# Loading one weight block from another engine's DMA queue, and reordering the first evictions, at the start of a Winograd-multiplied FFN kernel

## The chip, the cores and the metric

The kernel runs on one core of one Trainium2 chip. The metric is device time in microseconds (us) of one execution, the median of several runs. Engines are called as the profile does: PE (TensorE matmul), PEld (its weight loads), DVE (VectorE), ACT (ScalarE), POOL (GpSimd), SP (SyncE, which here only issues DMAs). "SPq" and "ACTq" are DMA issues on SP and on ACT.

## The reference, cut to what matters

```
xn = layernorm(x)                                   # x: 4 x 1024 x 1024, float32
g  = sigmoid(xn @ gate_w.T + gate_b); u_g = xn * g
s  = c * scan(b * u_g, tanh(a)) + (d + d_lr) * u_g  # d_lr from the mean of u_g over time
p  = softmax(xn @ wr.T); top 2 of 8; gates = p / sum
h  = silu(xn @ w1.T); h = silu(h @ w3.T); h = h @ w2.T
f[index_k] += gate_k * h       for the two choices k  # index_k is 0 to 7: a row of the output
out = x + s * silu(f)
```

The indices run from 0 to 7, so `f` differs from zero only in the first eight rows. The kernel computes the whole of `h` up to `silu(h @ w3.T)`, sums it by index, and applies `w2` to the eight sums; all other rows of `out` are copies of `x`.

## The kernel before, in words

Every product of a 1024x1024 weight with a unit of 1024 tokens is done with seven block products of 512x512 instead of eight, in sums and differences of blocks (the scheme of Strassen and Winograd). A unit `n` is 0 to 8: 0 to 3 multiply by `w1`, 4 by `gate_w`, 5 to 8 by `w3`. A product `i` of a unit is four tiles `j` of 128 rows, each accumulated in a bank of PSUM (`main0` to `main4`) over four slices `k`.

Each float32 factor is split in a high part, a rounded copy in the type float32r (`h..`, `wh..`, made on ACT), and a low part, the difference (`l..`, `wl..`, made on DVE). A product then is three matmuls, high by high, low by high and high by low: lines 995, 996 and 997, in `three`. So before PE can multiply anything, ACT must have copied and DVE subtracted.

The order of the work on all engines comes from one list, `steps`, written out by hand for the start and filled from a table afterwards. Each engine walks the same list and takes the steps that are its own, in that order, with semaphores between engines. DMA issues are steps, too: in the kernel before, all loads of the start are issued by SP (lines 717 to 734).

The steps around the change, all at the start, in unit 0:

- `WARM`: PE transposes the identity 34 times into the bank `spare` (line 1004); the results are not used.
- `ROW r`: SP loads 128 tokens, 512 KB, a "token tile" `r` (line 723). Tiles 0 and 1 go to `wh6f`, 2 and 3 to `wh5f`, 4 and 5 to `rows`, 6 and 7 to `wh4f`.
- `W0 k`: SP loads slice `k` of the first block of w1 (W11), 256 KB, into `wl2f` (line 726). `WL`: it loads a whole block, 1 MB (line 734).
- `NA`, `NB`: mean and variance of a token tile on DVE (1184 to 1186), the root on POOL, then the normalisation on DVE (1190). `NS` takes the mean and variance on ACT instead (859 to 861), for tiles 4 and 7.
- `TR t`: PE transposes a normalised tile in eight pieces (1014): four into one bank, four into another, `TE t,h` then evicts each of the two banks on ACT with two copies, high part (871) and float32 (873), and `TL t,h` makes the low part of it on DVE (1147, `x3r` and `x5r`).
- `WH0 k`: ACT makes the high part of slice `k` of W11 (877, `wh0r`), `WO0 k`: DVE its low part (1147, `wl0r`).
- `MP half,k`: PE multiplies two token tiles (256 columns) by slice `k` of W11: 12 matmuls. `MP 0,k` needs `WO0 k` and both `TL 0,0` and `TL 1,0`; `MP 1,k` needs `TL 3,0`.

From then on (`MM`, 512 columns each) PE has one product behind the other.

Of the kernel before, what the change touches and what calls it, by code (L numbers as in the profile page):

```python
# [5 lines left out]
P = 128  # L6
# [82 lines left out]
def plan():  # L89
# [7 lines left out]
    for n in range(NN):  # L97
# [93 lines left out]
        if 0 < n < GATE:  # L191
# [4 lines left out]
            for t, (m, i, j) in enumerate(when):  # L196
# [4 lines left out]
                if t % 4 == 3:  # L201
                    k = 4 * i + j
# [32 lines left out]
        if n >= GATE:  # L235
            for r in range(8):
                s = 8 * (n - GATE) + r
# [9 lines left out]
    for k in range(3):  # L247
# [7 lines left out]
    at(NN - 1, 6, 3, "FM", 0)  # L255
    at(NN - 1, 6, 3, "FM", 1)

    steps = [("WARM", 0), ("ROW", 0), ("ROW", 1)] + [("W0", k) for k in range(4)] + [("ROW", 2), ("ROW", 3), ("WL", 0, 6, "12"),
             ("ROW", 4), ("ROW", 5), ("ROW", 6), ("ROW", 7), ("WL", 0, 5, "21"), ("WL", 0, 4, "22"), ("CST", 0),
# [106 lines left out]
def program(nc, x, xT, wB, w2T, small, out):  # L366
    steps = plan()
# [14 lines left out]
    for s in steps:  # L382
        if s[0] == "XL":
            q = place[s[1:]]
# [25 lines left out]
    with ExitStack() as ctx:  # L410
# [33 lines left out]
        ident = sb("ident", [P, P])  # L444
# [17 lines left out]
        def w_f(p, part):  # L462
            return W[p][part][0][:, :, :]
# [29 lines left out]
        main = [ps(f"main{i}", [P, HT]) for i in range(BANKS)]  # L493
        lgp = [ps(f"lgp{i}", [P, HT]) for i in range(2)]
        spare = ps("spare", [P, HT])
# [6 lines left out]
        s_id = sem("s_id")  # L502
# [15 lines left out]
        s_w0 = [sem(f"s_w0{k}") for k in range(4)]  # L518
# [192 lines left out]
        @block.sync  # L711
        def _(eng):
            wait = Waiter(eng)
            ncopy = 0
            for s in steps:
                kind = s[0]
                if kind == "ROW":
                    r = s[1]
                    if r >= 10:
                        wait(s_st2, r - 9)  # L720
                    elif r >= 8:
                        wait(s_tr, 2 * (r - 3))
                    eng.dma_start(row_buf(r), x[r * P:(r + 1) * P, :]).then_inc(s_row[r if r < 8 else 4 + r % 2], 16)
                elif kind == "W0":
                    k = s[1]
                    eng.dma_start(w_f(2, 1)[:, k, :], wB[0, 0, 0, :, k, :]).then_inc(s_w0[k], 16)
                elif kind == "CST":
                    eng.dma_start(cst[:, :], small).then_inc(s_cst, 16)
                elif kind == "WL":
                    w, p, b = s[1:]  # L730
                    if w:
                        g = 7 * ((GATE, L2)[w - 1] - 1) + p
                        wait(s_mm, done(g))
                    eng.dma_start(w_f(p, 1), wB[w, int(b[0]) - 1, int(b[1]) - 1]).then_inc(s_wl[p], 16)
                elif kind == "XL":
                    n, b = s[1:]
                    kh, h = BLK[b]
                    vacated(wait, n, b)
                    if n < GATE:
                        src = xT[n, kh, h]  # L740
                    elif n == GATE:
                        wait(s_xs["acbd".index(b)], 16)
                        src = xh_d[kh, h]
                    else:
                        for j in range(4):
                            c_gone(wait, n - L2, AT_OF[(kh, h)], j)
                        src = H_d[n - L2, kh, h]
                    eng.dma_start(xf(n, b), src).then_inc(s_pl[loads[(n, b)][0]], 16)
                elif kind == "XS":
                    b = s[1]  # L750
                    raw_in(wait, 0, b)
                    kh, h = BLK[b]
                    eng.dma_start(xh_d[kh, h], xf(0, b)).then_inc(s_xs["acbd".index(b)], 16)
                elif kind == "MV":
                    wait(s_mvs, nth(*s))
                    eng.dma_start(mv_d[s[1]].rearrange("r (t p) -> (r t) p", p=P), mvs[:, :]).then_inc(s_mvd, 16)
                elif kind == "BC":
                    n, h = divmod(s[1], 2)
                    wait(s_mvd, 16 * nth("MV", s[1]))
                    if n > 1:  # L760
                        wait(s_ln, nth("LN", n - 1, "cd"[h]))
                    eng.dma_start(bcs[h][:, :, :], mv_d[s[1]].partition_broadcast(P)).then_inc(s_bc[h], 16)
                elif kind == "GL":
                    k = nth(*s) - 1
                    n, i, j = s[1:]
                    if k < 4:
                        wait(s_st2, 24)
                    else:
                        wait(s_gx, k - 3)
                    o, h = OUT_OF[i]  # L770
                    eng.dma_start(xt[:, k % 4, :], xh_d[o, h, :, j, :]).then_inc(s_xt[k % 4], 16)
                elif kind == "CP":
                    r0, r1 = max(E, s[1] * P), (s[1] + 1) * P
                    eng.dma_start(out[r0:r1, :], x[r0:r1, :]).then_inc(s_cp, 16)
                    ncopy += 1
                elif kind == "X8":
                    wait(s_oz, 1)
                    for q in range(NQ):
                        eng.dma_start(x8[rows8[q], :], x[0:E, q * QC:(q + 1) * QC]).then_inc(s_x8, 16)
                elif kind == "W2":  # L780
                    wait(s_mm, done(7 * (NN - 1) + 1))
                    for r in range(2):
                        eng.dma_start(w2f[:, 4 * r:4 * r + 4, :],
                                      w2T.rearrange("(k p) n -> p k n", p=P)[:, 4 * r:4 * r + 4, :]).then_inc(s_w2, 16)
            wait(s_fin, 1)
            for q in range(NQ):
                eng.dma_start(out[0:E, q * QC:(q + 1) * QC], fin[rows8[q], :]).then_inc(s_out, 16)
            wait(s_cp, 16 * ncopy)
            wait(s_out, 16 * NQ)
# [58 lines left out]
        def _(eng):  # L848
            wait = Waiter(eng)
# [12 lines left out]

            for s in steps:
                kind = s[0]
                if kind == "TE":
                    t, h = s[1:]
                    wait(s_tr, 2 * nth("TR", t) - 1 + h)
                    bk = tr_banks(t)[h][:, :].rearrange("p (k t) -> p k t", t=P)
# [5 lines left out]
                elif kind == "WH0":  # L874
                    k = s[1]
# [57 lines left out]
                elif kind == "ST":  # L933
# [3 lines left out]
                    q = s_ss[j] if i == 6 else s_sg[j] if i == 4 else s_su[j]  # L937
# [5 lines left out]
                elif kind == "STAT":  # L943
                    r = s[1]
                    k, h, t = nth(*s), r // 4 % 2, r % 4
# [45 lines left out]
        def _(eng):  # L991
# [7 lines left out]
            for s in steps:  # L999
                kind = s[0]  # L1000
                if kind == "WARM":
                    wait(s_id, 1)
                    for q in range(34):
                        eng.transpose(spare[:, q % 4 * P:(q % 4 + 1) * P], ident[:, :], ident[:, :])
                    wait(s_id, 2)
                elif kind == "TR":
                    t = s[1]
# [468 lines left out]
```

## Time and profile before

| | us |
|---|---|
| median of 3 runs | 775.17 |
| the three runs | 774.08, 775.17, 776.29 |
| the profiled execution, its own time | 776.75 |
| its span | 774.8 |
| PE busy | 756.1 (98%) |
| DVE busy | 510.9 (66%) |
| ACT busy | 347.4 (45%) |
| start of the first product (`MP 0,0`) | 15.43 |
| start of the fifth (`MP 1,0`) | 27.42 |

The profiled execution's own time holds its span and some 2 us around it. PE is busy nearly all the time, so time is to be had only where PE waits or runs slowly, and both happen in the first 28 us. "PEclk" is the clock that TensorE was granted: 1.00 is 2.4 GHz, 0.50 is 1.2 GHz. DMA rows give the packets of each queue: q1 is SP's, q10 ACT's.

### The profile page before, as it was taken

How to read it: one execution, taken by the hardware profiler on the slowest of the kernel's cores; microseconds unless marked ns; L12 is line 12 of the kernel's file. 1: busy time of each engine (PE TensorE's matmuls, PEld its weight loads, DVE VectorE, ACT ScalarE, POOL GpSimd, SP SyncE). 2: the span in 40 equal slices, each digit the busy share in tenths (PEclk: the TensorE clock that was granted, in tenths of full speed). 3: DMA queues.
4: the chain of work that ended last, by engine and by line, in shares of the span. 5: the costliest groups of instructions: out<-in, count | busy, mean ns of one | idle time of the engine just before them, and what ended most of it. 6: DMA issues, size and time to landing. Idle time of an engine off the chain costs nothing.

```text
span 774.8 us, 8825 instructions
## 1 busy us (share of the span) xinstructions
PE 756.1 (98%) x3544; PEld 596.9 (77%) x3544; DVE 510.9 (66%) x567; ACT 347.4 (45%) x451; POOL 40.3 (5%) x52
## 2 busy tenths in 40 slices
PE   5999999999999999999989999999999999999996
PEld 5868877887788787888878878778777778777773
DVE  5789789675958487557999998565534552455322
ACT  4769964835572434242834354225122332234121
POOL 3300103020302000000000000000000000000000
PEclk8999999999999999999999999999999999999999
DMA  8743774536442533566495613221230323010500
GB/s 333 273 164 139 239 236 162 203 137 213 154 150 95 191 136 123 217 207 254 155 384 174 273 47 135 110 113 78 109 136 28 162 110 135 1 55 2 217 1 3
DMA packets 27401, 117.21 MB, mean 151 GB/s; under 512 B 3440, under 2 KB 3680, under 8 KB 20320
## 3 DMA queue, kind: packets, MB, share of 16 engines
q1 hardware_dynamic: 18144, 99.87, 35.7%
q10 hardware_dynamic: 9216, 16.78, 5.8%
q8 instruction: 28, 0.46, 0.2%
q14 instruction: 13, 0.11, 0.0%
HBM read 95.60 MB, written 37.77 MB: 172 GB/s over the span
## 4 chain that ended last, share of the span: by engine, by line
PE 85%; DVE 8%; issue 3%; DMA 2%; ACT 2%; SPq 0%; DVEq 0%
PE main L995 27%; PE main L997 26%; PE main L996 26%; PE lgp L1061 2%; DMA wl6f<-wB 1%; PE spare L1088 1%; DMA wl2f<-wB 1%; PE lgp L1088 1%; DVE x3r L1147 1%; DVE s L1147 1%; DVE x3f L1147 1%; DVE x0r L1147 1%; DVE x1r L1147 1%; DVE u L1379 1%; PE main L1122 0%
## 5 line engine op out<-in xcount | busy, mean ns | idle before, releaser
L1147 DVE TENSOR_TENSOR s<-s,main 128x512 f32<-128x512 f32 x72 | 48.7, 682 | 62.7 <-PE main L997 62.6
L1147 DVE TENSOR_TENSOR u<-u,main 128x512 f32<-128x512 f32 x36 | 24.5, 685 | 49.5 <-PE main L997 49.5
L931 ACT ACTIVATE u<-u 128x512 f32<-128x512 f32 x32 | 20.1, 631 | 57.2 <-DVE u L1147 57.1
L931 ACT ACTIVATE s<-s 128x512 f32<-128x512 f32 x32 | 20.0, 630 | 52.5 <-DVE s L1147 52.5
L1147 DVE TENSOR_TENSOR u<-s,main 128x512 f32<-128x512 f32 x32 | 21.7, 682 | 29.6 <-PE main L997 29.6
L931 ACT ACTIVATE rows<-rows 128x512 f32<-128x512 f32 x16 | 10.1, 631 | 67.9 <-DVE rows L1147 67.8
L912 ACT ACTIVATE s<-main 128x512 f32<-128x512 f32 x36 | 20.5, 594 | 44.5 <-PE main L997 19.0
L1147 DVE TENSOR_TENSOR rows<-s,main 128x512 f32<-128x512 f32 x16 | 11.0, 687 | 31.2 <-PE main L997 31.2
L861 ACT ACTIVATE rows<-rows,nm 128x1024 f32<-128x1024 f32 x24 | 27.7, 1154 | 0.8
L859 ACT ACTIVATE rows<-rows 128x1024 f32<-128x1024 f32 x25 | 26.2, 1046 | 2.0 <-DMA rows<-x 1.8
L931 ACT ACTIVATE u<-main 128x512 f32<-128x512 f32 x32 | 18.6, 590 | 17.6 <-PE main L997 17.4
L995 PE MATMUL main<-x2r,wh0r 128*128 128x256 f32 (+1 forms) x48 | 16.8, 349 | 6.6 <-DVE x3r L1147 6.6
L997 PE MATMUL main<-x2r,wl0r 128*128 128x256 f32 (+1 forms) x48 | 16.3, 340 | 0.0
L995 PEld LDWEIGHTS main<-x2r,wh0r 128*128 128x128 f32 x48 | 10.2, 212 | 7.7 <-DVE x3r L1147 7.1
L845 POOL MEMSET tail<- 128x1024 f32 x1 | 1.0, 955 | 269.1 <-PE main L997 269.1
L833 POOL TENSOR_SCALAR mvu<-acs 128x4 f32<-128x4 f32 x6 | 5.0, 827 | 188.0 <-ACT rows L861 188.0
L996 PE MATMUL main<-x4r,wh4r 128*128 128x512 f32 x32 | 13.0, 406 | 0.0
L995 PE MATMUL main<-x6r,wh3r 128*128 128x512 f32 x32 | 12.5, 392 | 0.0
L996 PE MATMUL main<-x6r,wh0r 128*128 128x512 f32 x32 | 12.5, 390 | 0.0
L996 PE MATMUL main<-x5r,wh1r 128*128 128x512 f32 x32 | 12.5, 390 | 0.0
L997 PE MATMUL main<-x6r,wl3r 128*128 128x512 f32 x32 | 12.5, 389 | 0.0
L996 PE MATMUL main<-x5r,wh2r 128*128 128x512 f32 x32 | 12.5, 389 | 0.0
(699 smaller groups left out, 2440.0 us busy)
## 6 DMA issues: line engine op xcount, KB each, us to landing
out<-x SPq DMA_DIRECT2D x31, 512.0 KB, 7.3
rows<-x SPq DMA_DIRECT2D x26, 512.0 KB, 4.1
H_d<-u ACTq DMA_DIRECT2D x32, 256.0 KB, 4.3
H_d<-s ACTq DMA_DIRECT2D x16, 256.0 KB, 3.2
rows<-xh_d SPq DMA_DIRECT2D x16, 256.0 KB, 4.9
w2f<-w2T SPq DMA_DIRECT2D x2, 2048.0 KB, 10.5
wl6f<-wB SPq DMA_DIRECT2D x3, 1024.0 KB, 8.3
wl4f<-wB SPq DMA_DIRECT2D x3, 1024.0 KB, 7.3
```

Of the source, the lines that this page charges most:

```text
L833: eng.tensor_scalar(mvu[:, h, 0, :], acs[:, h, 0, :], 1.0 / D, None, ALU.mult)
L859: link(eng.activation(row, row, ACT.Copy, accum_out=total))
L861: return eng.activation(where, row, ACT.Square, bias=nm[:, 0:1], accum_out=square)
L912: eng.activation(s1[:, j, :], bk, ACT.Copy).then_inc(s_pa, 1)
L931: ins = eng.activation(dst, src, ACT.Silu)
L995: eng.matmul(o, sh, mh, start=first, stop=False, skip_group_check=True)
L996: eng.matmul(o, sh, ml, start=False, stop=False, skip_group_check=True)
L997: return eng.matmul(o, sl_, mh, start=False, stop=last, skip_group_check=True)
L1061: ins = eng.matmul(lgp[h][Q * q:Q * (q + 1), :], wr32[:, NQ * kh + q, :], xf(n, b)[:, q, :], start=(kh == 0), stop=(kh == 1))
L1088: ins = eng.matmul(acc[o][Q * j:Q * (j + 1), :], Pz[:, 8 * u + 4 * h + j, :], c_buf(n, i, j), start=(u == 0 and h == 0), stop=(u == NU - 1 ...
L1147: return eng.tensor_tensor(o, a, b, op)
L1379: ins = eng.scalar_tensor_tensor(buf, buf, 1.0, xt[:, k % 4, :], ALU.add, ALU.mult, accum_out=us[:, h, e:e + 1])
```

## The change

Three things change, all in the first steps.

1. The four `W0` loads are issued by ACT instead of SP, after a wait for the end of POOL's last preparation (`s_id` at 2, after `iota`). SP issues the token tiles right behind one another.
2. The order of ACT and DVE work: `WH0 2` and `WH0 3` go behind evictions, the low parts go between the `TL`, `NA 2` goes behind `TL 1,0`, and `TR 2` goes behind `MP 0,2`.
3. PE transposes the identity 38 times instead of 34 at the start, and 12 times more behind `TR 1`, into `main0`.

```diff
-    steps = [("WARM", 0), ("ROW", 0), ("ROW", 1)] + [("W0", k) for k in range(4)] + [("ROW", 2), ("ROW", 3), ("WL", 0, 6, "12"),
+    steps = [("WARM", 0)] + [("W0", k) for k in range(4)] + [("ROW", 0), ("ROW", 1), ("ROW", 2), ("ROW", 3), ("WL", 0, 6, "12"),
              ("ROW", 4), ("ROW", 5), ("ROW", 6), ("ROW", 7), ("WL", 0, 5, "21"), ("WL", 0, 4, "22"), ("CST", 0),
-             ("NA", 0), ("NA", 1), ("NB", 0), ("TR", 0), ("NB", 1), ("TR", 1),
-             ("WH0", 0), ("WH0", 1), ("WH0", 2), ("WH0", 3), ("TE", 0, 0), ("WO0", 0), ("TL", 0, 0), ("NA", 2), ("TE", 1, 0), ("TL", 1, 0),
-             ("TE", 0, 1), ("TE", 1, 1), ("WO0", 1), ("WO0", 2), ("NA", 3), ("NB", 2), ("WO0", 3),
-             ("MP", 0, 0), ("MP", 0, 1), ("TR", 2), ("MP", 0, 2), ("MP", 0, 3), ("NA", 5), ("NB", 3), ("TR", 3),
+             ("NA", 0), ("NA", 1), ("NB", 0), ("TR", 0), ("NB", 1), ("TR", 1), ("WARM", 1),
+             ("WH0", 0), ("WH0", 1), ("TE", 0, 0), ("WO0", 0), ("TL", 0, 0), ("WH0", 2), ("TE", 1, 0), ("WO0", 1), ("TL", 1, 0),
+             ("WH0", 3), ("TE", 0, 1), ("TE", 1, 1), ("NA", 2), ("WO0", 2), ("NA", 3), ("WO0", 3), ("NB", 2),
+             ("MP", 0, 0), ("MP", 0, 1), ("MP", 0, 2), ("TR", 2), ("MP", 0, 3), ("NA", 5), ("NB", 3), ("TR", 3),
...
-                elif kind == "W0":
-                    k = s[1]
-                    eng.dma_start(w_f(2, 1)[:, k, :], wB[0, 0, 0, :, k, :]).then_inc(s_w0[k], 16)
...
+                if kind == "W0":
+                    k = s[1]
+                    wait(s_id, 2)
+                    eng.dma_start(w_f(2, 1)[:, k, :], wB[0, 0, 0, :, k, :]).then_inc(s_w0[k], 16)
...
-                    for q in range(34):
-                        eng.transpose(spare[:, q % 4 * P:(q % 4 + 1) * P], ident[:, :], ident[:, :])
+                    idle = main[0] if s[1] else spare
+                    for q in range(12 if s[1] else 38):
+                        eng.transpose(idle[:, q % 4 * P:(q % 4 + 1) * P], ident[:, :], ident[:, :])
```

How the instructions stand on ACT, from the program's start, before the change (`wh0r<-wl2f` are the high parts of W11, the rows with `main`, `lgp` and `spare` the evictions of token tiles 0 and 1):

```order
L877 ACT_TABLE_LOAD
L877 ACTIVATE wh0r<-wl2f 128x512 x4
L871 ACTIVATE x2r<-main 128x4x128
L873 ACTIVATE x0f<-main 128x4x128
L871 ACTIVATE x2r<-lgp 128x4x128
L873 ACTIVATE x0f<-lgp 128x4x128
L871 ACTIVATE x4r<-lgp 128x4x128
```

And with the change:

```order
L865 DMA wl2f<-wB 128x512 x4
L878 ACT_TABLE_LOAD
L878 ACTIVATE wh0r<-wl2f 128x512 x2
L872 ACTIVATE x2r<-main 128x4x128
L874 ACTIVATE x0f<-main 128x4x128
L878 ACTIVATE wh0r<-wl2f 128x512
L872 ACTIVATE x2r<-lgp 128x4x128
L874 ACTIVATE x0f<-lgp 128x4x128
L878 ACTIVATE wh0r<-wl2f 128x512
L872 ACTIVATE x4r<-lgp 128x4x128
```

The four loads now stand ahead of everything on ACT, the load of the function table too, and two of the four high parts stand ahead of the first eviction instead of four.

DVE in the same place, from the normalisation of tiles 0 and 1 on, before:

```order
L1190 TENSOR_SCALAR wh6f<-wh6f,mv 128x1024 x2
L1147 TENSOR_TENSOR wl0r<-wl2f,wh0r 128x512
L1147 TENSOR_TENSOR x3r<-x0f,x2r 128x4x128
L1184 BN_STATS bst<-wh5f 128x6
L1185 BN_STATS bst<-wh5f 128x6
L1186 BN_AGGR mv<-bst 128x2
L1147 TENSOR_TENSOR x3r<-x0f,x2r 128x4x128
L1147 TENSOR_TENSOR wl0r<-wl2f,wh0r 128x512 x2
```

And with the change:

```order
L1192 TENSOR_SCALAR wh6f<-wh6f,mv 128x1024 x2
L1149 TENSOR_TENSOR wl0r<-wl2f,wh0r 128x512
L1149 TENSOR_TENSOR x3r<-x0f,x2r 128x4x128
L1149 TENSOR_TENSOR wl0r<-wl2f,wh0r 128x512
L1149 TENSOR_TENSOR x3r<-x0f,x2r 128x4x128
L1186 BN_STATS bst<-wh5f 128x6
L1187 BN_STATS bst<-wh5f 128x6
L1188 BN_AGGR mv<-bst 128x2
L1149 TENSOR_TENSOR wl0r<-wl2f,wh0r 128x512
```

The second `x3r` (`TL 1,0`) now stands ahead of the statistics of tile 2, behind the low part of the second slice.

SP from the program's start, with the change (before, the four `wl2f<-wB` stood between the first two rows):

```order
L723 DMA wh6f<-x 128x1024 x2
L723 DMA wh5f<-x 128x1024 x2
L731 DMA wl6f<-wB 128x2048
L723 DMA rows<-x 128x1024 x2
L723 DMA wh4f<-x 128x1024 x2
```

What stands behind W11's four pieces on SP before stands ahead of, or beside, them on the other queue now.

## Rows read from the trace of the kernel before

**Rows 1.** Waits of PE, whole span: us in total, times, longest us.
```profile
PE main L995 <- DVE x3r L1147: 6.6, 2, 5.1
```
**Rows 2.** Timeline, start to first product: start us, us, engine, line, operation.
```profile
8.35 0.81 DVE L1190 TENSOR_SCALAR wh6f<-wh6f,mv 128x1024 f32<-128x1024 f32 x1 [0.78 <-POOL mv L819]
...
9.71 0.60 PE L1014 MATMUL spare<-ident,wh6f 128*128 128x128 f32 x4
9.78 1.91 ACT L877 ACTIVATE wh0r<-wl2f 128x512 fp32r<-128x512 f32 x3 [1.22 <-DMA wl2f<-wB]
...
11.59 0.58 ACT L871 ACTIVATE x2r<-main 128x512 fp32r<-128x512 f32 x1
...
13.02 0.61 ACT L873 ACTIVATE x0f<-lgp 128x512 f32<-128x512 f32 x1
13.29 0.69 DVE L1184 BATCH_NORM_STATS2 bst<-wh5f 128x6 f32<-128x512 f32 x1
...
14.73 0.64 DVE L1147 TENSOR_TENSOR x3r<-x0f,x2r 128x512 fp32r<-128x512 f32 x1
...
15.43 0.58 PE L995 MATMUL main<-x2r,wh0r 128*128 128x256 f32 x1 [5.12 <-DVE x3r L1147]
```
**Rows 3.** Windows: engines' busy us, then PEclk, DMA share, GB/s.
```profile
0.00:4.50 4.50, 2.90 (x14) 2.90 (x15) 0.53 (x1) 1.28 (x1) 1.65 (x13) 1.00 0.58 224
...
14.00:15.00 1.00, 0.00 (x0) 0.00 (x0) 0.97 (x3) 1.00 (x4) 0.10 (x1) 0.91 0.98 406
15.00:21.50 6.50, 6.07 (x28) 6.07 (x29) 6.43 (x13) 3.18 (x7) 3.51 (x5) 0.50 1.04 424
```
**Rows 4.** Chain in order of time, from low clock to fifth product: start us, us, what.
```profile
20.49 0.21 PE main L996
...
22.33 0.12 PE main L996
...
25.08 0.45 PE lgp L1014 x4
...
27.42 0.39 PE main L995
```
**Rows 5.** Timeline of issues and of tile 4's statistics, and landing of W11's pieces.
```profile
1.67 1.85 SPq L726 DMA_DIRECT2D wl2f<-wB  x4
...
2.77 0.14 POOL L804 IOTA iota<- 128x8 f32 x1
...
17.37 1.06 ACT L859 ACTIVATE rows<-rows 128x1024 f32<-128x1024 f32 x1 [1.79 <-DMA rows<-x]
...
19.84 0.19 ACT L861 ACTIVATION_READ_ACCUMULATOR wh3f<-rows,nm 128x1 f32 x1
...
DMA to landing us min/median/max: 6.2/7.7/7.9
```
**Rows 6.** ACT's queue alone: timeline of an issue; its queue from 113.0 to 113.4; its landing.
```profile
112.24 0.33 ACTq L938 DMA_DIRECT2D H_d<-s  x1
q10 hardware_dynamic: 59, 0.12, 79.0%
H_d<-s ACTq DMA_DIRECT2D x1, 256.0 KB, 2.4
```
**Rows 7.** ACT's queue beside SP's: issue and landing; queues from 51.0 to 51.5.
```profile
46.80 0.34 ACTq L938 DMA_DIRECT2D H_d<-u  x1
H_d<-u ACTq DMA_DIRECT2D x1, 256.0 KB, 6.5
q1 hardware_dynamic: 22, 0.18, 85.5%
q10 hardware_dynamic: 25, 0.05, 26.4%
```
**Rows 8.** Again: an issue; ACT's queue from 302.5 to 303.0, its first packets.
```profile
300.13 0.35 ACTq L938 DMA_DIRECT2D H_d<-u  x1
q10 hardware_dynamic: 16, 0.03, 16.8%
```

More of the change, by code:

```diff
@@ L864, in _ @@
                 kind = s[0]
-                if kind == "TE":
+                if kind == "W0":
+                    k = s[1]
+                    wait(s_id, 2)
+                    eng.dma_start(w_f(2, 1)[:, k, :], wB[0, 0, 0, :, k, :]).then_inc(s_w0[k], 16)
+                elif kind == "TE":
                     t, h = s[1:]
```

## The prediction

> **What bounds the kernel now.** I read the waits of PE first, since PE is busy for 98% of the span: its longest wait, by far, is the one for a low part made by DVE at the start, 6.6 us in two pieces, one of 5.1 [rows 1]. The timeline shows the long piece: PE ends the transposes of tile 1 at 10.3 and starts `MP 0,0` at 15.43, when `TL 1,0` on DVE is done [rows 2]. Follow that back. `TL 1,0` stands behind the statistics of tile 2 (13.29 to 14.73), though its input was there when ACT ended at 13.63. ACT in turn began the evictions only at 11.59, behind four high parts of W11, three of which waited for a DMA until 9.78. So two things hold the start: the arrival of W11, and work put ahead of what PE needs. The windows show a second loss: the granted clock is 0.91 between 14 and 15 and 0.50 from 15 to 21.5, the lower level, 1.2 GHz [rows 3]. It fell at about 14.8, some 4.5 us after PE's last transpose. At that level a matmul of 256 columns takes 0.21 us, afterwards 0.12 [rows 4]. From 27.42 on PE is fed, but for short waits, and the order of work there is unchanged; so I take the start of `MP 1,0` as the place where the change is cashed, and add its shift to the profiled execution's 776.75.
>
> **What the clock costs before.** With the clock high, PE would do the first 24 matmuls in 2.9 us instead of 5.3. Then `TR 2` has its tile only at 18.7, `MP 0,2` and `MP 0,3` end at 22.5, and 1.45 (a batch of 12 matmuls is 12 x 0.12) aside, the tail from the middle of `TR 3` to `MP 1,0` is as before 1.9 (25.53 to 27.42, rows 4): about 24.7 instead of 27.4. So the low clock is worth 2.7 us there. The three runs of before lie between 774.08 and 776.29, 2.2 us apart, and 776.75 - 2.7 = 774.05. I read that as: the profiled execution had the low clock, and the runs do not all have it. I therefore give times on the profiled execution's scale, and do not subtract the 1.58 us by which it lies above the median of 775.17. A difference of 0.3% is 2.3 us; less than that a measurement of this kernel can't tell from no change.
>
> **The change, part by part.**
>
> *Issue.* ACT waits for POOL's `iota`, done at 2.91 [rows 5], then issues four loads at 0.33 each or somewhat more [rows 6, 7], done by 4.6 at the latest; the function table's load follows, 1.28 of ACT busy in the first window [rows 3], and ends by 6. It all lies ahead of the first landing of a piece, before 1.67 + 6.2 = 7.9 [rows 5]: cost nothing, unless a piece landed before 6. SP is rid of four issues (1.85), so its own loads go out earlier.
>
> *First packet.* The trace of before has no load on ACT's queue, only stores of the same size, 256 KB. Alone, one is issued at 112.24 and its packets flow at 113.0 (0.8 us later) and it lands after 2.4 [rows 6]. Beside SP transfers its first packets show 4.3 us after issue (46.80, then 51.0) and 2.4 us after (300.13, then 302.5), and the first of these lands after 6.5 [rows 7, 8]. The ends are 0.8 and 4.3. Here SP's queue holds four token tiles and a block, so the busy rows are nearest; I take 3.1: first packets at 6.0.
>
> *Shares.* Where both queues are busy, they move 22 and 25 packets in half a microsecond [rows 7], one for one. But a packet of W11's pieces, like one of these stores, holds 2 KB, a token tile's 4 KB, a whole block's 8 KB (0.18 MB in 22). By 6.0 SP's queue has moved 1.0 MB by 4.5 (224 GB/s) and 0.6 more at 0.41 MB per us, of the 2.1 MB of tiles 0 to 3; 116 packets of 4 KB are left. Piece 0: 116 pairs of 6 KB and 12 of 10 KB, 0.84 MB, 2.0 us, to 8.0. Piece 1 goes beside the block `wl6f`: 116 pairs of 10 KB and 12 of 6 KB, 1.26 MB, 3.1 us, to 11.1. Pieces 2 and 3 go beside tiles 4 and 5, 1.9 us each, to 13.0 and 14.9. A landing follows the mean of the bytes: before, the fourth piece landed at about 11.0 and its bytes were through at 9.0, 2 us; alone on ACT's queue it is 0.8 behind the last full window [rows 5, 6]. I take 1.4: landings at 9.4, 12.5, 14.4 and 16.3, against 7.9, 9.8, some 10.3 and 11.0 before. The loads of tiles 2 and 3 come earlier, and nobody waits for them.
>
> *The rule on queues.* ACT's queue moved packet for packet with SP's [rows 7]. By this rule the trace agrees: the Trainium skill, "DMA: Bandwidth & Descriptors", section "Queues, rings and completion order", says that each DMA engine takes turns between the queues it has work for, packet by packet. The same page, section "Issuing engines are not separate DMA queues", says that issuing from several engines only saves the issuing sequencer's time; by that the arrivals of W11 would stay as they are, which is a rival below.
>
> *New order on ACT and DVE.* Copies on ACT follow one another at 0.48, the last 0.15 longer (four from 11.59 to 13.63, rows 2). `WH0 1` starts at 12.5, `TE 0,0` ends at 14.1, `WH0 2` starts at its landing, 14.4, `TE 1,0` runs from 14.9 to 16.0, `TL 1,0` takes 0.7: `MP 0,0` at 16.7, 1.3 us later than before. Moving `NA 2` behind saves 1.1 by itself (13.63 to 14.73), and with one high part fewer ahead of `TE 1,0` another 0.5; the late pieces eat both.
>
> *Idle transposes.* Four more at the start take 0.45 (four in 0.45, rows 4); even if all of that showed on tile 0's transposes, ACT's first eviction waits for W11's second piece until 13: nothing, and 0.45 at most if the pieces come early. Twelve more behind tile 1's, 1.3 us, end at 11.6, before any start of `MP 0,0` that I find: nothing. They cut PE's idle from 6.4 to 5.1 us. The fall came 4.5 after the last transpose; by that it would come at 16.1, against a start at 16.7. That is a toss-up. I take the clock as kept, slightly, for the spread of the runs says that an idle of this length, 5.1 us before as well, doesn't always cost it.
>
> *From there on.* Clock kept: the first three batches end at 18.2, 19.6 and 21.1. DVE does `NA 2` (1.44), `WO0 2`, `NA 3`, `WO0 3` (0.6 each) and `NB 2` (0.8) behind `TL 1,0`, to 21.6. `TR 2` then to 22.5, `MP 0,3` to 23.95, half of `TR 3` to 24.4, the tail 1.9: 26.3, 1.1 earlier than 27.42. Clock low: 24 matmuls to 22.0, the clock back some 6.3 after the start as before, `MP 0,2` to 23.9, `TR 2` to 24.8, `MP 0,3` to 26.2, `TR 3` and tail: 28.5, 1.1 later.
>
> **The sum** with the clock kept: 776.75 - 1.1 = 775.6. With the clock low: 777.9.
>
> **The rivals.**
>
> *Pieces as early as before.* If moving the queue leaves the arrivals alone, only the new order counts: `WH0 1` at 9.78, `TE 1,0` to 12.8, `MP 0,0` at 13.5, an idle of 1.9 and no low clock. Then something else is late next: tile 4, which landed at 17.37. ACT's `NS 4` ends at 20.0 [rows 5], then `TE 2` (two pairs) and `TE 3,0` to 23.0, `TL 3,0` to 23.7: 3.7 earlier, 773.05. If ACT's queue starts within a microsecond, as alone, the pieces land at 9.3, 12.2 and 14.0, `MP 0,0` starts at 14.5, and it comes to nearly the same, 24.0. For it: SP's queue is only just filling when ACT issues. Against it: two of two busy rows.
>
> *Pieces later still, and slower than before.* The place is the queues at 7.3 (2.97 + 4.3, the late end): SP's tiles are through by then, and piece 0 goes beside `wl6f`, 3.2 us, the others 1.9 each. With 2 us to landing, piece 1 is there at 14.4 and piece 2 at 16.3; `MP 0,0` at 18.6, PE idle for 7 us, the clock surely low: 3.0 later, 779.75. It decides from a landing of piece 2 after about 15.5.
>
> **How the numbers follow.** Late pieces, as worked out: 0.5, a little more than half of it with the clock kept (own range 774.3 to 778). Early pieces: 0.37. Very late: 0.13. Faster by more than 0.3% means below 772.85: a little under half of the early case and a bit of the first, 0.2. Slower means above 777.5: most of the very late case and a third of the low-clock half, 0.17. The rest, 0.63, is within. The range takes in the early case with half a microsecond to spare and the low clock: 772.3 to 778.2; the very late end is left out.
>
> **What would show it.** First packets on q10 at 6 and not 4; `WH0 1` at 12.5; `MP 0,0` at 16.7; `MP 1,0` at 26.3 with the clock at 1.00 throughout, or 28.5 with a stretch of 0.50. Wrong it is if all four pieces have landed by 11 (early), or the first after 11 (very late), or if PE waits anew behind 30 us.

## Result and the profile after

| | before | after |
|---|---|---|
| median of the runs | 774.65 (6 runs, 774.08 to 776.29) | 778.37 (6 runs, 777.32 to 779.09) |
| profiled execution, own time / span | 776.75 / 774.8 | 778.95 / 777.1 |
| start of `MP 0,0` | 15.43 | 18.43 |
| start of `MP 1,0` | 27.42 | 29.89 |

The ratio is 1.0044, 95% interval 1.0031 to 1.0056: slower by 0.44%, 3.7 us between the medians and 2.3 between the two profiled spans. The waits of PE in the changed kernel (us in total, times, longest us):

```profile
PE main L996 <- DVE x3r L1149: 8.0, 2, 6.6
PE main L996 <- DVE u L1149: 2.0, 1, 2.0
```

The wait for a low part is 8.0 us instead of 6.6, its long piece 6.6 instead of 5.1 [rows 1]. The second row is a wait that ends at 405.66 and that before has too, at 403.33; behind 30 us no wait is new. So the loss lies at the start. The timeline of the changed kernel there (start us, us, engine, line, operation, and in brackets the idle time before and what ended it):

```profile
2.95 2.32 ACTq L865 DMA_DIRECT2D wl2f<-wB  x4
10.39 1.47 PE L1006 MATMUL main<-ident 128*128 128x128 f32 x12
12.09 0.63 ACT L878 ACTIVATE wh0r<-wl2f 128x512 fp32r<-128x512 f32 x1 [5.50 <-DMA wl2f<-wB]
14.04 0.63 ACT L878 ACTIVATE wh0r<-wl2f 128x512 fp32r<-128x512 f32 x1 [1.33 <-DMA wl2f<-wB]
14.58 0.58 ACT L872 ACTIVATE x2r<-main 128x512 fp32r<-128x512 f32 x1
16.04 0.63 ACT L878 ACTIVATE wh0r<-wl2f 128x512 fp32r<-128x512 f32 x1 [0.40 <-DMA wl2f<-wB]
17.06 0.59 ACT L874 ACTIVATE x0f<-lgp 128x512 f32<-128x512 f32 x1
17.68 0.69 DVE L1149 TENSOR_TENSOR x3r<-x0f,x2r 128x512 fp32r<-128x512 f32 x1 [0.71 <-ACT x0f L874]
17.98 0.63 ACT L878 ACTIVATE wh0r<-wl2f 128x512 fp32r<-128x512 f32 x1 [0.34 <-DMA wl2f<-wB]
18.43 0.58 PE L996 MATMUL main<-x2r,wh0r 128*128 128x256 f32 x1 [6.56 <-DVE x3r L1149]
```

Read it from the end. `MP 0,0` waits for `x3r` at 17.68, that for the eviction at 17.06, and ACT came to the evictions of tile 1 only behind the third high part, which waited for its DMA until 16.04. Each of the four high parts waited for a DMA; in before the last three started together at 9.78 [rows 2]. PE stood ready from 11.86 (10.39 + 1.47). The queues of the changed kernel from 6.0 to 6.5, from 6.5 to 7.0, from 8.0 to 8.5 and from 10.0 to 10.5 (packets, MB, share of 16 engines), then its windows (engines' busy us, PEclk, DMA share, GB/s):

```profile
q1 hardware_dynamic: 58, 0.18, 96.2%
...
q1 hardware_dynamic: 37, 0.14, 71.0%
q10 hardware_dynamic: 14, 0.03, 35.7%
...
q1 hardware_dynamic: 22, 0.09, 66.2%
q10 hardware_dynamic: 11, 0.02, 23.9%
...
q1 hardware_dynamic: 19, 0.16, 77.1%
q10 hardware_dynamic: 19, 0.03, 17.5%
```

```profile
6.50:9.50 3.00, 2.75 (x26) 2.52 (x24) 2.09 (x4) 0.08 (x1) 1.48 (x3) 1.00 0.98 291
9.50:12.00 2.50, 2.37 (x20) 2.13 (x20) 0.00 (x0) 0.00 (x0) 0.00 (x0) 1.00 1.02 410
16.00:17.00 1.00, 0.00 (x0) 0.00 (x0) 0.97 (x2) 0.96 (x2) 0.00 (x0) 0.88 1.05 414
17.00:23.00 6.00, 4.58 (x21) 4.58 (x22) 5.25 (x10) 5.60 (x12) 2.14 (x4) 0.50 1.04 426
23.00:24.00 1.00, 1.00 (x8) 1.00 (x7) 1.00 (x3) 0.10 (x2) 0.51 (x1) 0.71 0.89 340
405.00:410.00 5.00, 4.34 (x12) 3.42 (x13) 4.97 (x19) 0.00 (x0) 0.00 (x0) 0.66 0.64 259
```

ACT's queue moves nothing before 6.5, though its first load was issued at 2.95. For two microseconds it then gets half as many turns as SP's (56 packets beside 108, from 6.5 to 8.5), and from 8.5 to 11.5 as many (131 beside 129). From 6.5 to 9.5 the engines are as busy as ever (0.98) but move 291 GB/s, against 410 behind it. The clock is granted in full until PE has stood idle for nearly 5 us, then 0.50 from about 16.8 to 23.6. And there is a second stretch of low clock, at 405 to 410, which I had not looked for; before has it as well, so PE does not run slowly in the first 28 us only:

```profile
403.00:408.00 5.00, 4.67 (x13) 3.69 (x14) 4.97 (x23) 0.00 (x0) 0.00 (x0) 0.66 0.59 243
```

### The profile page after: what moved, and what is told of

It is laid out like the page before. It is cut to its first block, busy times and chain, and to the rows that moved or that the text cites. A ratio compares the mean times of both kernels' runs of the same rounds, so it can differ in the third digit from the quotient of the medians.

```text
span 777.1 us, 8857 instructions
## 1 busy us (share of the span) xinstructions
PE 757.9 (98%) x3560; PEld 599.1 (77%) x3560; DVE 511.1 (66%) x567; ACT 347.3 (45%) x451; POOL 40.2 (5%) x52
## 4 chain that ended last, share of the span: by engine, by line
PE 85%; DVE 8%; issue 3%; DMA 3%; ACT 2%; POOL 0%; ACTq 0%; SPq 0%; DVEq 0%; POOLq 0%
PE main L996 27%; PE main L997 26%; PE main L998 26%; PE lgp L1063 2%; DMA wl2f<-wB 2%; DMA wl6f<-wB 1%; PE spare L1090 1%; PE lgp L1090 1%; DVE s L1149 1%; DVE x3f L1149 1%; DVE x0r L1149 1%; DVE x1r L1149 1%; DVE x3r L1149 1%; DVE u L1381 1%; PE main L1124 0%
## 5 line engine op out<-in xcount | busy, mean ns | idle before, releaser
L996 PE MATMUL main<-x2r,wh0r 128*128 128x256 f32 (+1 forms) x48 | 16.8, 349 | 8.0 <-DVE x3r L1149 8.0
L996 PEld LDWEIGHTS main<-x2r,wh0r 128*128 128x128 f32 x48 | 10.2, 213 | 9.1 <-DVE x3r L1149 8.5
L996 PE MATMUL main<-x6r,wh3r 128*128 128x512 f32 x32 | 12.5, 392 | 0.0
L997 PE MATMUL main<-x6r,wh0r 128*128 128x512 f32 x32 | 12.5, 390 | 0.0
L997 PE MATMUL main<-x5r,wh1r 128*128 128x512 f32 x32 | 12.5, 390 | 0.0
L998 PE MATMUL main<-x6r,wl3r 128*128 128x512 f32 x32 | 12.5, 390 | 0.0
L997 PE MATMUL main<-x5r,wh2r 128*128 128x512 f32 x32 | 12.5, 389 | 0.0
```

The costliest lines, as they stand in the source:

```text
L996: eng.matmul(o, sh, mh, start=first, stop=False, skip_group_check=True)
L997: eng.matmul(o, sh, ml, start=False, stop=False, skip_group_check=True)
L998: return eng.matmul(o, sl_, mh, start=False, stop=last, skip_group_check=True)
```

## The experiments

Theory A, "late pieces": the new order and the idle transposes are sound, and the loss is the queue, since ACT's queue starts late and then has a packet's turn for a packet of SP's. Rival B: the new order or the twelve idle transposes cost time themselves. Open too was why W11's first packets move slowly. The before of each comparison ran on the same chip; its medians are 774.93 to 775.28, and 774.65 in the comparison above, so a difference of some 0.6 us between kernels of different comparisons tells nothing.

**The change taken apart.** The first kernel ("order-only") is the changed one with W11's loads back on SP's queue, in their place behind tile 1; the second ("queue-only") is before with only the queue changed. The diff (cut to the list of steps; the issue moves from ACT's code to SP's with it) is that of order-only; queue-only has it the other way round:

```diff
- steps = [("WARM", 0)] + [("W0", k) for k in range(4)] + [("ROW", 0), ("ROW", 1), ("ROW", 2), ...
+ steps = [("WARM", 0), ("ROW", 0), ("ROW", 1)] + [("W0", k) for k in range(4)] + [("ROW", 2), ...
```

> W11's four pieces issued by SP again, between token tiles 1 and 2 as before the change; the new order on ACT and DVE and the idle transposes stay. Queue theory (the change lost by moving the queue, and its new order is good): the pieces land at about 7.9, 9.8, 10.3 and 11.0 as before, the first product starts at 13.5 and the fifth at 23.7, clock at 1.00 throughout, and every run lies near 773.0, some 0.2% under the median of before. Rival, order theory (high parts put between evictions hold up ACT, or the later low parts starve the third product): the fifth product starts no earlier than 24.7, where before's would with a high clock, and the time is 774.6 or more.

> The kernel before with one thing changed: the four pieces are issued by ACT behind the wait for iota. Queue theory: the pieces land as in the changed kernel (12.1, 14.0, 16.0, 18.0), and since all four high parts stand ahead of the first eviction in the old order, the first product starts at about 22.3 instead of 15.4, the clock is low then, the fifth starts at about 34, and the time is 781 to 784, 0.9 to 1.1% over before. Order theory: most of the loss was the order's, so this kernel stays within 1 to 2 us of before, 775 to 777.

The order alone: 773.62 us, ratio 0.9984 (0.9974 to 0.9994). The queue alone: 781.88, ratio 1.0083 (1.0069 to 1.0096). First products of both, and their fifth:

```profile
12.59 0.38 PE L995 MATMUL main<-x2r,wh0r 128*128 128x256 f32 x1 [0.79 <-DVE x3r L1148]
23.70 0.58 PE L995 MATMUL main<-x2r,wh0r 128*128 128x256 f32 x1 [1.50 <-DVE x3r L1148]
```

```profile
22.36 0.58 PE L996 MATMUL main<-x2r,wh0r 128*128 128x256 f32 x1 [11.98 <-DVE x3r L1148]
33.70 0.39 PE L996 MATMUL main<-x2r,wh0r 128*128 128x256 f32 x1 [1.46 <-DVE x3r L1148]
```

A holds, B falls: against before's 775.07 on that chip the order gives 1.4 us and the queue takes 6.8. Together they cost 3.7 and not 5.4: with the new order three late pieces, and not four, stand ahead of the evictions that PE waits for, and `MP 0,0` is at 18.43 and not 22.36. In the order-only kernel `MP 1,0` is 3.7 us earlier than in before, but its span only 2.2 (772.6) and its median 1.4. Its clock fell at the fifth product instead, behind waits of PE no longer than 1.28 and 1.50 us, and from there to 400 us it needs 1.5 us more than before does (377.42 from `MP 1,0` to the wait of 2 us, for 375.91):

```profile
24.00:27.00 3.00, 3.00 (x15) 3.00 (x15) 3.00 (x6) 1.66 (x1) 0.80 (x1) 0.50 0.94 384
```

**Idle transposes.** The changed kernel with 66 behind tile 1's own instead of 12, and the order-only kernel with 34 and none instead of 38 and 12 (only the numbers in `range(12 if s[1] else 38)` change):

> The changed kernel with 66 idle transposes behind tile 1's instead of 12, so that PE is busy until about 17.7 and the first product, which still starts at about 18.4, finds the clock high in every run. Clock theory (part of the changed kernel's loss is the low clock, which half of its runs have): clock at 1.00 from 12 on, the fifth product at 27.8 instead of 29.9, all runs within 0.5 us of 777.0 and none near 779. Rival (the two groups of runs have another cause): two groups 1.6 us apart as before, median 778.4.

> The order-only kernel without the added idle transposes (34 at the start and none behind tile 1's). If the idle transposes matter once the pieces are early: PE then is idle from about 10 to 12.6, the clock is low more often, and the median is 1 us over the order-only kernel's 773.6. If not, as I expect for an idle of 2.4 us: within 0.4 us of it, and the whole gain of the order-only kernel is the order's.

With 66 the changed kernel takes 777.16 (ratio 1.0025, 1.0014 to 1.0036), and the clock stays at 1.00 through all of the first products:

```profile
10.22 7.37 PE L1006 MATMUL main<-ident 128*128 128x128 f32 x66
18.00 0.39 PE L996 MATMUL main<-x2r,wh0r 128*128 128x256 f32 x1 [0.42 <-DVE x3r L1149]
27.58 0.39 PE L996 MATMUL main<-x2r,wh0r 128*128 128x256 f32 x1 [1.47 <-DVE x3r L1149]
```

From `MP 0,0` to `MP 1,0` it is 9.58 us with the clock at 1.00 and 11.46 in the changed kernel: the low clock costs 1.9 us here. The spread that I expected to go with it stays: the seven executions lie between 775.71 and 777.76. Without any added idle transposes and W11 on SP's queue the time is 773.41 (0.9981, 0.9973 to 0.999), the same as with them: once the pieces are early, 12 buy nothing.

**ACT's wait and W6.** The changed kernel without the wait for `iota` ahead of the four issues, and the changed kernel with W6's first block issued behind tile 7, so that pieces meet tiles of 4 KB packets only:

```diff
                 if kind == "W0":
                     k = s[1]
-                    wait(s_id, 2)
```

> The changed kernel without the wait for iota: ACT issues the four pieces from about 0.8 us on, together with SP's first token tiles. If the first packets of ACT's queue come late because SP's queue has been filled before it, they now come at about 1.8 and the pieces land at 6 to 9; token tile 0 lands 1 us and tile 1 up to 2 us later, the first product starts at about 13.0 to 13.5, the fifth at 23.7, and the time is 773.0. Rival, ACT's queue is served after SP's whenever both are busy: the first packets come at 5 or later, the first product at 17 or later, and the time stays above 777.

> The changed kernel with the block wl6f issued behind token tile 7 instead of behind tile 3, so that W11's pieces never share with packets of 8 KB. Sharing packet for packet: while the pieces move, half a microsecond of q10 holds about 35 packets instead of 17 to 27, the first piece lands at about 11, the last at 16.5, the first product starts at 17.2, 1.2 us earlier than in the changed kernel, and the time is 1 to 2 us less, 776 to 777.5. Rival, a fixed delay of ACT's queue (its transfers wait for what SP issued before, whatever the size): landings and time as in the changed kernel, 12 to 18 and 778.4.

Without the wait: 773.36 (0.9974, 0.9965 to 0.9983). ACT issues at 0.74, its first packets show between 2.0 and 2.5, and the pieces land at 6.1, at 8.7 and, the last two, before ACT comes to them. The slow packets now fall on the first tiles: tile 0 landed at 5.90 instead of 3.97, PE stands idle for 2.08 before its transposes, and yet `MP 0,0` starts at 14.60 and `MP 1,0` at 24.18. So the change is worth having on ACT's queue as well, if it is issued ahead of SP's backlog: the wait of 2.2 us alone turns 773.4 into 778.4. With W6 late: 777.26 (1.0023, 1.0011 to 1.0035), high parts at 10.24, 12.37, 14.33 and 16.28, `MP 0,0` at 16.71. Out of the way of W6's 8 KB packets `MP 0,0` is 1.7 us earlier than in the changed kernel, 1.3 earlier than with 66 idle transposes (18.00), whose loads are the changed kernel's, and the time is 1.1 less. The queues from 10.0 to 10.5 show the turns: one for one again, but nearly twice as many as the 19 beside W6:

```profile
q1 hardware_dynamic: 35, 0.14, 65.8%
q10 hardware_dynamic: 36, 0.07, 37.8%
```

**The slow spell.** In before too the DMA engines move little while W11's first packets are under way: 142 GB/s from 4.5 to 6.5. Is it the first access to that memory? A load of 256 bytes from W11, issued on ACT's queue ahead of all else, was added to the changed kernel. Is it the form of the pieces, whose rows are 2 KB of each 8 KB? In the version that beats both (next part), W11 was loaded as one transfer, and as two; the diff shows the issue of the one transfer:

```diff
-                    eng.dma_start(w_f(2, 1)[:, k, :], wB[0, 0, 0, :, k, :]).then_inc(s_w0[k], 16)
+                    if s[1] == 0:
+                        eng.dma_start(w_f(2, 1), wB[0, 0, 0]).then_inc(s_w0[0], 16)
```

> The changed kernel with one small load more, issued by ACT first of all, at 0.7: 16 rows of 16 bytes from W11's megabyte, 64 KB apart, into a tile nobody reads. In every run so far the DMA rate falls to a third or two thirds for 2 us when the first packets of W11's first piece move. If that is the first access to that memory, it is now over before the piece comes: 290 GB/s and less between 6.5 and 9.5 become some 380, the pieces land 1 to 1.5 us earlier (11, 13, 15, 16.8), the first product starts at 17.2, and the time is 777.2. Rival (it is the pieces' 2 KB rows, or the start of any transfer on a queue): landings and time as in the changed kernel.

> W0's pieces replaced by one transfer of 1 MB (rows of 8 KB) on SP's queue behind tile 1, with W6 behind tile 6. It tells what makes the DMA engines slow while W11's first packets move. If it is the 2 KB rows of the four pieces, the rate between 4.5 and 6.5 us goes from 143 GB/s to near 400 and all of W11 has landed by 7.5 to 8.0. If it is W11's memory or the place in time, the rate stays below 250 GB/s in those 2 us and W11 lands at 9.0 to 9.5. In both cases all four evictions wh0r have to wait for the whole, so ScalarE takes them one after the other, and MP 0,0 starts about 1.5 to 4 us after the landing, at 11.5 to 13.8; the time is then 770.5 to 772.5, against 771.6 with four pieces.

> W11 as two transfers of 512 KB (rows of 4 KB) on SP's queue behind tile 1, with W6 behind tile 6. If 2 KB rows alone are slow, the rate from 4.5 to 6.5 is near 400 GB/s as with 8 KB rows (397), and the halves land at about 8.2 and 9.6; the first eviction x2r starts at 9.3 instead of 10.2, MP 0,0 at 12.6 to 13.2 and MP 1,0 at 22.7 to 23.1, a time of 770.8 to 771.8. If rows of 4 KB are slow too (they have half the stride's bytes unread between them), the rate is 200 to 300 GB/s and it comes to the four pieces' 771.6 or above.

The early touch changes nothing that lies outside the spread: 777.15 (1.0031, 1.002 to 1.0042), with 324 GB/s from 6.5 to 9.5, while the kernel with 66 idle transposes and no touch had 330; the first three pieces were there for ACT at 10.87, 13.42 and 15.39, and without the touch at 11.08, 13.64 and 15.62. The form of the transfers does change the rate. Windows from 4.5 to 6.5 with four pieces (the order below), two, and one:

```profile
4.50:6.50 2.00, 2.00 (x21) 2.00 (x20) 1.95 (x5) 0.00 (x0) 0.77 (x2) 1.00 0.70 143
```

```profile
4.50:6.50 2.00, 2.00 (x21) 2.00 (x20) 1.97 (x5) 0.00 (x0) 0.64 (x2) 1.00 0.94 264
```

```profile
4.50:6.50 2.00, 2.00 (x15) 2.00 (x14) 1.97 (x5) 0.00 (x0) 0.66 (x2) 1.00 0.99 397
```

And the queue's packets from 5.5 to 6.0 in the same three:

```profile
q1 hardware_dynamic: 27, 0.05, 82.9%
```

```profile
q1 hardware_dynamic: 25, 0.10, 87.5%
```

```profile
q1 hardware_dynamic: 25, 0.20, 96.8%
```

25 to 27 packets in half a microsecond whatever they hold, 2, 4 or 8 KB: a packet took 0.25 to 0.31 us (27 packets in 0.829 x 16 x 0.5 us, 25 in 0.968 x 16 x 0.5). A microsecond later, from 7.0 to 7.5, 90 packets of 2 KB pass in the first of these kernels, in 0.10 us each. So at first a packet of W11's costs about the same time whatever its size, and small rows pay for it; packets of 8 KB take it at the full rate too (25 in 0.968 x 16 x 0.5 us between 11.0 and 11.5 in the changed kernel). The later pieces have the same 2 KB rows and are fast, so the rows alone are not the cause. What makes the first ones dear isn't settled: that it is the first access to W11 is not supported, though the touch reached only 256 bytes of its megabyte. A higher rate is also not an earlier start: as one transfer W11 was there for ACT at 9.18, and not at 7.5 to 8.0 as expected, and all four high parts wait for the whole.

The test on the changed kernel itself, W11 as one transfer of 8 KB rows on ACT's queue:

> The changed kernel with W11 as one transfer of 1 MB (rows of 8 KB) on ScalarE's queue instead of four of 2 KB rows. If the changed kernel's four landings at 12.1 to 18.0 come from two things, the slow spell of 2 KB rows at the start and the share per packet (a 2 KB packet for each 4 or 8 KB packet of SP), both go: the rate between 6.5 and 9.5 rises from 291 GB/s to near 400, W11's 128 packets go one for one with tiles of 4 KB and then W6 of 8 KB (1.5 to 2 MB, 3.7 to 5 us from 6.5 on) and it lands whole at 11.8 to 13.3; MP 0,0 starts at 16.0 to 17.5 instead of 18.43, MP 1,0 at about 28.0, and the median is 776 to 777.3. If the spell hangs on ScalarE's queue or on the place in time, the rate stays near 291, W11 lands after 14, MP 0,0 starts after 18.4 and the time is 778.4 or more.

```profile
4.50:6.50 2.00, 2.00 (x18) 2.00 (x17) 1.97 (x5) 0.15 (x1) 0.82 (x2) 1.00 0.93 328
6.50:9.50 3.00, 2.48 (x22) 2.04 (x21) 1.83 (x4) 0.00 (x0) 1.25 (x2) 1.00 1.03 418
17.02 0.58 PE L996 MATMUL main<-x2r,wh0r 128*128 128x256 f32 x1 [5.42 <-DVE x3r L1149]
28.45 0.39 PE L996 MATMUL main<-x2r,wh0r 128*128 128x256 f32 x1 [1.47 <-DVE x3r L1149]
```

The dip is gone (418 against 291 GB/s), W11 lands whole at 12.6, `MP 0,0` is 1.4 us earlier. The time is 777.41 (1.0024, 1.0014 to 1.0035), 1.0 below the changed kernel and 0.1 above the range that I gave. With the same one transfer on SP's queue and W6 late the time is 771.76; the 5.6 us between the two are the queue and W6's place together. Late W6 gave 1.1 with four pieces, so most of it should be ACT's queue, but no run has the one without the other.

**A version that beats both.** W11's pieces on SP's queue behind tile 1, the change's order, and W6's block behind tile 6:

```diff
+             ("ROW", 4), ("ROW", 5), ("ROW", 6), ("WL", 0, 6, "12"), ("ROW", 7),
```

> The order-only kernel (pieces issued by SP) with the block wl6f issued behind token tile 6 instead of behind tile 3. Queue theory, next bound: in the order-only kernel, tiles 4 and 5 landing at 16.4 and 18.8 are what is late next; they now land 2.5 us earlier, DVE's wait of 1.6 for tile 5 and PE's of 1.3 go, and the fifth product starts at 22.2 instead of 23.7: about 772 against 773.6. Rival (the DVE and ACT work from there on is the bound, not the arrival): the fifth product at 23.3 or later and 773.3 or more. A second rival: wl6f, landing at 18.5, is late for its high part, and PE waits anew behind 30 us.

> W0's pieces on SP's queue, W6 behind token tile 6, and 28 idle transposes instead of 12 behind tile 1's own, about 2 us more of them in the stretch before the first product. If the granted clock falls in some executions because TensorE stands idle there, it stays at 1.00 until MP 0,0 at about 13.5 to 13.8 in the profile, MP 1,0 starts by 23.9, no execution is above 772.5 and the median is 771.0 to 771.3, a part of a us under the same kernel with 12. If the clock's fall is owed to the waits inside the first products, MP 1,0 stays at 23.7 to 24.5, the clock falls there as before in some executions, and the median stays at 771.6. Idle transposes that last past x3r's arrival would push MP 0,0 beyond 13.9 and cost that much.

It takes 771.6 (0.9957, 0.9943 to 0.997). Tile 4 was late in the order-only kernel, as the prediction's early rival had it; here it isn't. It was expected with `MP 1,0` at 22.2; its profile has it at 24.55, with the clock at 0.50 from 14.6 to 18.0, and is with 772.97 an execution 1.4 above the median. One transfer for W11 (771.76, 0.9957) and two (771.72, 0.9957, 0.9944 to 0.997) give the same median, with `MP 1,0` at 23.15 and 22.13 in their profiles. What is won there does last to 400 us: the product behind the wait of 2 us starts at 400.43, 399.04 and 398.21 in the three. With two transfers 1.1 of it goes at the very end: there the clock falls at 762.1, 8 us before the end, and in the other two only in the last 3 us.

Sixteen more idle transposes did not help; the kernel is slower with them: 773.34 (0.9977, 0.9968 to 0.9986). Its profile and that of the one-transfer kernel, from the same chip, agree to `MP 1,0`, 23.20 and 23.15, and stand 2.3 us apart at the end (spans 771.9 and 769.6). 1.4 of the 2.3 are there before the clock falls, through a block load for a later product, which came late in this one profile of fourteen (DVE takes it 9.6 us after its issue, and 8.2 to 8.6 after in the others). DVE, then PE, in the kernel with 28 idle transposes, and the same two in the one-transfer kernel:

```profile
360.72 2.29 DVE L1148 TENSOR_TENSOR wl6f<-wl6f,wl2f 128x2048 f32<-128x2048 f32 x1 [6.78 <-DMA wl6f<-wB]
400.41 0.50 PE L995 MATMUL main<-x7r,wh4r 128*128 128x512 f32 x1 [1.99 <-DVE u L1148]
```

```profile
359.36 2.29 DVE L1148 TENSOR_TENSOR wl6f<-wl6f,wl2f 128x2048 f32<-128x2048 f32 x1 [5.47 <-DMA wl6f<-wB]
399.04 0.50 PE L995 MATMUL main<-x7r,wh4r 128*128 128x512 f32 x1 [1.99 <-DVE u L1148]
```

The other 0.9 comes behind it, where the windows from 400 to 410 differ in the clock. Whether the kernel's other executions are slower for the same two reasons is not known.

```profile
400.00:410.00 10.00, 9.59 (x35) 7.74 (x36) 9.74 (x35) 1.34 (x2) 0.00 (x0) 0.83 0.34 126
```

```profile
400.00:410.00 10.00, 10.00 (x45) 8.13 (x45) 9.70 (x38) 2.06 (x3) 0.00 (x0) 1.00 0.27 96
```

## Why the prediction was right and wrong

The forecast was 775.6, between 772.3 and 778.2; it came to 778.37, 0.2 above the range, and slower by more than 0.3%, to which I gave 0.17. The result lies between my case of late pieces and that of very late ones; by my own sign, the first landing after 11, it was the very late one.

*Right.* ACT's queue beside a busy SP queue starts late (6.5; I took 6.0) and from 8.5 on goes packet for packet: the pieces come late, not early. `MP 0,0` follows the third landing as worked out, 2.4 us behind it (I had 2.3). The length of the first products was right at both clocks: 9.6 us and 11.8 forecast, 9.58 and 11.46 measured. The early rival was sized right up to `MP 1,0`: 23.7 forecast, 23.70 in the order-only kernel, with tile 4 late as said. Where the queue was moved and nothing else, four late landings cost 6.8 us. The Trainium skill, "DMA: Bandwidth & Descriptors", section "Issuing engines are not separate DMA queues", says that issuing from several engines saves only the sequencer's time for the issue. The runs disagree: which queue, and when, decided when the data came. The Trainium skill, "DMA: Bandwidth & Descriptors", section "Queues, rings and completion order", has each DMA engine take turns between the queues, packet by packet. The rows from 10.0 to 10.5 agree (19 and 19, and 35 and 36 with W6 late); those from 6.5 to 8.5 do not look like it (108 and 56).

*Wrong: the landings.* "landings at 9.4, 12.5, 14.4 and 16.3" became 12.1, 14.0, 16.0 and 18.0. The first piece's 2.7 us split up: its packets began 0.5 later; its passage took 3.7 us (6.5 to about 10.2, when ACT's queue had moved 128 packets by the counts of half microseconds) instead of 2.0; and it landed 1.9 behind its bytes, not 1.4. The middle term is the large one. I worked it out at a full 0.41 MB per us and at one turn of SP's for each of ACT's, while 291 GB/s passed and SP's queue had 176 packets from 6.5 to 10.0 beside ACT's 122; and the trace of before already showed 142 GB/s from 4.5 to 6.5 with W11's pieces on SP's queue. I read the window up to 4.5 and the one from 14 on, and none between. The piece on which `MP 0,0` hangs, the third, is 1.6 late by this, and `MP 0,0` 1.7 (18.43 for 16.7). About 1 us of the first piece's lateness may be of this execution: the queue-only kernel and the one with 66 idle transposes issue the same loads, and had it at 11.04 and 11.08 (the third at 16.02 and 15.62).

*Wrong: the clock.* "That is a toss-up. I take the clock as kept, slightly", with the spread of before's runs as the reason. PE stood idle for 6.6 us, and the clock was low from 16.8 on. The reason doesn't hold: nearly all executions of before seem to have the low clock at the start. The evidence is the mean granted clock of each execution. Before's profile has three stretches at 0.50: 14.8 to 21.4, 403.9 to 407.3, and the last 2 us, when PE has no work left. Together they make its mean of 0.992; without the second it would be 0.994, without the first 0.996. Of before's 79 executions in the four later comparisons 32 have 0.992 and take 776.0 us in the mean, 34 have 0.994 and take 774.6, 6 have 0.993, and 7 have 0.996 and take 774.1. So, by this estimate, only these 7 lacked the stretch at the start, and the larger part of the spread goes with the one at 403 to 408, at which I had not looked. Seven of the fourteen profiles here have it (the changed kernel's too), seven don't, always behind the same wait of 2.0 us, which all fourteen have. From the product behind that wait to a wait near the end it is 362.4 us with the stretch and 361.5 without: 0.9 us; the rest of the 1.4 between the two groups isn't explained.

With the clock kept and my own landings `MP 1,0` was to start at 26.3. It started 3.6 later: 1.7 by the landings and 1.9 by the clock. Had I taken the low clock with my own landings, the sum would have been 777.9; with `MP 1,0` at 29.89 it is 776.75 + 2.5 = 779.2, against the profiled 778.95.

*Wrong: the scale.* The forecast of a median was made on the scale of one profiled execution, which lies 2.1 above before's median of six runs. After's profiled execution lies 0.6 above its own. This error hid part of the others: 1.1 us off before's median would have been a forecast of some 773.6, and the miss 4.8 us instead of 2.8. That the result lies only 0.2 outside the range is luck to this extent. The mean clocks split the 3.7 us between the medians, too. Three of the changed kernel's six executions have 0.992 and take 779.0, three have 0.994 and take 777.5. Against before's groups of the same clock, from the later comparisons, that is 3.0 and 2.9 us: about 2.9 are the change, and the other 0.8 are the mix of executions (estimates, across chips). The two profiled executions are only 2.2 apart; before's lies 0.7 above the mean of its group.

*Wrong: the chances.* The case that made it slower needed two things together, a landing beyond 15.5 and the low clock. I gave the pair 0.13 although the second follows from the first; and the half in which the pieces are late with the low clock stood at 777.9 already, next to the bound of 777.5. Slower should have had about a third.

## What to carry to other kernels

A load that is wanted early doesn't come early by being moved to an idle queue. Issued 2.2 us behind another queue's backlog it started late here, and from then on got its turns by the packet, so that rows of 2 KB beside rows of 8 KB get a fifth of the bytes. What helps is to issue it ahead of the backlog (773.4 instead of 778.4), or to take a large block out of its way: W6 behind the tiles, on one queue, with the new order of the evictions, gave 3.3 us where the second queue took 3.7. And before the spread of runs is put down to one place, look for the granted clock over the whole span, and set each execution's time beside its mean clock. A single profile is one execution out of that spread, and its `MP 1,0` may stand for a median or not.

## What the runs showed of the hardware

- A second queue's first packets: at least 3.5 us after issue beside SP's full queue (2.95, then 6.5 or later), and at most 1.8 where SP had only just begun (0.74, then 2.0 to 2.5).
- Two busy queues: 56 packets beside 108 in the second queue's first 2 us (6.5 to 8.5), then one for one (131 beside 129 from 8.5 to 11.5).
- Between 5.5 and 6.0 W11's packets took 0.25 to 0.31 us each whether they held 2, 4 or 8 KB, and 0.10 for 2 KB between 7.0 and 7.5. From 4.5 to 6.5 rows of 4 and 8 KB made the rate 264 and 397 GB/s instead of 143.
- The clock fell in the order-only kernel at 23.7 to 27, with PE's waits before it no longer than 1.28 and 1.50 us. Behind a wait of 2.0 us at 398 to 410, which all fourteen profiles have, it fell in seven and stayed at 1.00 in seven; where it fell, the way from there to a wait near the end took 0.9 us longer (362.4 for 361.5).
- The same 1 MB load, issued at the same place of the program, was there for DVE 8.2 to 8.6 us after issue in thirteen profiles and 9.6 after in one, and PE was 1.4 us later for it 40 us on.
